# A selective scan layer whose preparation runs in halves of channels and tokens, with loads waited for later and the last sums ahead of the output products

## The reference

```python
x = x + _L2_attn_ref(_layernorm(x), ...)     # _L2_attn_ref adds its input too:
residual = x
xn = layernorm(x) * ln_w + ln_b
x_inner, z = split(xn @ W_in.T)              # 256 channels each
u = silu(causal_conv4(x_inner) + conv_b)     # 4 taps along 64 tokens of a sequence
dt_low, B_ssm, C_ssm = split(u @ W_x.T)      # 64 + 16 + 16
dt = clip(softplus(dt_low @ W_dt.T + b_dt) + 0.001, 0.001, 0.1)
h_t = exp(-dt_t * exp(log_A)) * h_{t-1} + dt_t * u_t * B_t   # 16 states a channel
y = sum_n(h * C) + u * D_param
return (y * silu(z)) @ W_out.T + residual
```

## Time and profile before

| what | us |
|---|---|
| median of three timed runs (3036.95 to 3038.14) | 3037.8 |
| profiled execution, device time | 3035.6 |
| its span | 3033.8 |
| the scan layer in it, from its first instruction to the last write of `x` | 2196.7 to 2490.3 |
| its loop, from the first scan | 2303.3 to about 2475 |

### The profile page before, as it was taken

One profiled execution on the slowest core, in us unless ns is written; L12 is line 12 of the kernel. 1 busy time (PEld: TensorE's weight loads), 2 busy tenths in 40 slices (PEclk: granted clock), 3 DMA queues, 4 the chain that ended last, 5 costly groups with the idle time before them and its releaser, 6 DMA issues. The chain is left out here.

```text
span 3033.8 us, 66495 instructions
## 1 busy us (share of the span) xinstructions
...
## 2 busy tenths in 40 slices
...
DMA packets 73344, 189.00 MB, mean 62 GB/s; under 512 B 12130, under 2 KB 39717, under 8 KB 73008
## 3 DMA queue, kind: packets, MB, share of 16 engines
...
q0 software_dynamic: 1024, 1.85, 0.2%
...
## 5 line engine op out<-in xcount | busy, mean ns | idle before, releaser
L3062 DVE CUSTOM_DVE_ANT_0 L_xattn_junk<-L_xattn_ps_mx,L_xattn_shift 128x512 f32<-128x512 f32 (+1 forms) x1024 | 545.1, 570 | 112.3 <-issue 102.1
L3143 ACT ACTIVATE L_xattn_pT<-L_xattn_ps_st 128x512 f32<-128x512 f32 x768 | 417.0, 594 | 402.4 <-PE L_xattn_ps_st L2901 402.4
L2914 PE MATMUL L_xattn_ps_mx<-L_xattn_kT,L_xattn_qb 32*128 32x512 f32 (+1 forms) x2048 | 480.0, 551 | 0.0
L2901 PE MATMUL L_xattn_ps_st<-L_xattn_qb,L_xattn_kT 32*128 32x256 f32 (+1 forms) x3328 | 454.5, 383 | 0.0
L3108 DVE TENSOR_TENSOR L_xattn_pT<-L_xattn_pT,L_xattn_capT 128x512 f32<-128x512 f32 (+1 forms) x710 | 423.2, 637 | 29.8 <-ACT L_xattn_pT L3143 26.8
L2901 PEld LDWEIGHTS L_xattn_ps_st<-L_xattn_qb,L_xattn_kT 32*128 32x128 f32 (+1 forms) x3328 | 299.3, 180 | 18.5
L2961 PE MATMUL L_xattn_ps_pv<-L_xattn_pT,L_xattn_v 128*17 128x128 f32 x6656 | 263.0, 276 | 0.0
L2961 PEld LDWEIGHTS L_xattn_ps_pv<-L_xattn_pT,L_xattn_v 128*17 128x17 f32 x6656 | 146.1, 96 | 163.3 <-issue 76.1
L2927 PE MATMUL L_xattn_ps_st<-L_xattn_less,L_xattn_ones_b 3*128 3x512 bf16 x768 | 177.8, 385 | 0.9 <-ACT L_xattn_pT L3143 0.7
L2868 POOL TENSOR_TENSOR L_xattn_qb<-ln_sq,L_xattn_four 128x256 f32<-128x256 f32 x32 | 19.6, 615 | 1089.0 <-PE L_xattn_ps_st L2901 1069.3
L2914 PEld LDWEIGHTS L_xattn_ps_mx<-L_xattn_kT,L_xattn_qb 32*128 32x128 f32 x2048 | 151.5, 183 | 23.9 <-DVE L_xattn_tops L3062 14.6
...
## 6 DMA issues: line engine op xcount, KB each, us to landing
...
```

The costliest lines, as they stand in the source:

```text
L2901: last = nc.tensor.matmul(st[0:chunk[j], w % 3, 256 * c2:256 * c2 + 256], kT[n % 3][r:r + 32, P * j:P * j + chunk[j]], qb[n % 3][r:r + 32, ...
L2914: last = nc.tensor.matmul(mx[:, w % 3, to:to + width], qb[n % 3][32 * g:32 * g + 32, 2 * (p % 2):2 * (p % 2) + 2, :].rearrange("p h q -> p ...
L3062: last = nc.vector.tensor_tensor_reduce(out=junk[:, w % 3, to:to + width], in0=mx[:, w % 3, to:to + width], in1=shift[:, k0:k0 + width], s ...
L3143: nc.scalar.activation(pT[b % HELD][:, :, gi, :], st[:, w % 3, :].rearrange("p (c k) -> p c k", c=2), ACT.Exp)\
```

## The change

The wait for the loads moves behind the first norm on ScalarE and DVE (PE's stays). The zero fill covers only the first column of each sequence, and `la` and `na` are made much later. All eight `xi` products come before the eight `z` products; DVE copies the first half of the channels, ScalarE the second. `CONV` cuts the convolution into three parts: the first half of the channels over all columns, the second half over columns 0 to 1023, and over the rest. PE runs 24 transposes whose result nobody reads, then the low-rank and step-size products for the first half of the tokens and for the second. Exp, Ln, the clips and the product with `u` go by halves of the tokens. The first two decays come after the first `xs`. At the end all sums stand ahead of the output products, and the skip and gate go in pieces of 512 columns. Which of the copies of `xbc` SP waits for changes with it; the loop is otherwise the same.

```diff
+        by_time = [(hf, i) for i in range(4) for hf in range(HALF)]
+        CONV = [(0, 0, TOK), (1, 0, TK), (1, TK, TOK)]
...
+            sp.wait_ge(*V.at("xbc3"))
+            sp.wait_ge(*A.at("xbc1"))
...
             pe.wait_ge(loaded, 160)
 
-            order = [(blk, i) for pair in (0, 1) for i in range(4) for blk in (pair, 2 + pair)]
-            for n, (blk, i) in enumerate(order):
+            for n, (hf, i) in enumerate(quads):
                 if n >= 4:
-                    pe.wait_ge(*(V.at(f"xi{(n - 4) // 2}") if blk < 2 else A.at(f"z{(n - 4) // 2}")))
-                nc.tensor.matmul(ps[:, (0 if blk < 2 else 2) + i % 2, :], win[:, P * blk:P * blk + P], hT[:, 512 * i:512 * i + 512],
+                    pe.wait_ge(*V.at(f"xi{n - 4}"))
+                nc.tensor.matmul(ps[:, n % 4, :], win[:, P * hf:P * hf + P], hT[:, 512 * i:512 * i + 512],
                                  start=True, stop=True).then_inc(PE.did(f"in{n}"), 1)
-            pe.wait_ge(*A.at("u1"))
-            for i in range(4):
+            for n, (hf, i) in enumerate(quads):
+                if n >= 4:
+                    pe.wait_ge(*A.at(f"z{n - 4}"))
+                nc.tensor.matmul(ps[:, 4 + n % 4, :], win[:, P * (2 + hf):P * (2 + hf) + P], hT[:, 512 * i:512 * i + 512],
+                                 start=True, stop=True).then_inc(PE.did(f"z{n}"), 1)
+            pe.wait_ge(*A.at("xi7"))
+            for _ in range(24):
+                nc.tensor.transpose(ps[:, 0, 0:P], c.ident[:, :], c.ident[:, :])
+
+            def low_rank(i):
...
-                    pe.wait_ge(*(A if i % 2 else V).at(f"xbc{i - 2}"))
+                    pe.wait_ge(*A.at(f"xbc{i - 2}"))
...
-            pe.wait_ge(*V.at("xbc2"))
...
+            def step_sizes(n):
+                hf, i = by_time[n]
                 if n >= 4:
                     pe.wait_ge(*V.at(f"pre{n - 4}"))
                 nc.tensor.matmul(ps[:, n % 4, :], wdt[:, P * hf:P * hf + P], xbc[0:R, 512 * i:512 * i + 512],
                                  start=True, stop=True).then_inc(PE.did(f"dt{n}"), 1)
+
+            pe.wait_ge(*A.at("u1"))
+            low_rank(0)
+            low_rank(1)
+            for n in range(4):
+                pe.wait_ge(*A.at(f"xbc{n // 2}"))
+                step_sizes(n)
+            pe.wait_ge(*A.at("u2"))
+            low_rank(2)
+            low_rank(3)
+            for n in range(4, 8):
+                pe.wait_ge(*V.at(f"xbc{n // 2}"))
+                step_sizes(n)
...
             total(K - 1, 0)
+            total(K - 1, 1)
             pe.wait_ge(*G.at("gate0_1"))
             pe.wait_ge(*V.at(f"scan{K - 1}_0"))
             out(0)
             out(1)
-            total(K - 1, 1)
-            pe.wait_ge(*V.at("gate1_1"))
+            pe.wait_ge(*V.at("gate1_1_0"))
             out(2)
+            pe.wait_ge(*V.at("gate1_1_1"))
             out(3)
...
         def _(dve):
-            dve.wait_ge(*A.at("la"))
-            nc.vector.tensor_scalar(na[:, :, :], la[:, :, :], -1.0, None, ALU.mult).then_inc(V.did("na"), 1)
-            nc.vector.memset(da[:, :, :, :], 0.0).then_inc(V.did("da_zero"), 1)
             ln_vector(c, dve, V, A, PE, tp, n1)
+            dve.wait_ge(loaded, 160)
             ln_vector(c, dve, V, A, PE, tp, n2)
...
+            nc.vector.memset(da[:, :, :, :].rearrange("p u h (b q) -> p (u h b) q", q=S)[:, :, 0:1], 0.0).then_inc(V.did("da_zero"), 1)
+            for n in range(4):
+                dve.wait_ge(*PE.at(f"in{n}"))
+                nc.vector.tensor_copy(xi[:, 0, 512 * n:512 * n + 512], ps[:, n, :]).then_inc(V.did(f"xi{n}"), 1)
+            dve.wait_ge(*V.at("xi3"))
+            for m, (hf, lo, hi) in enumerate(CONV):
+                if m == 1:
+                    dve.wait_ge(*A.at("xi7"))
+                x3, u3 = seq(xi[:, hf, lo:hi]), seq(cv[:, hf, lo:hi])
+                nc.vector.tensor_scalar(cv[:, hf, lo:hi], xi[:, hf, lo:hi], taps[:, hf, 3:4], cb[:, hf:hf + 1], ALU.mult, ALU.add)\
+                    .then_inc(V.did(f"cv{m}3"), 1)
...
-            for i in (0, 2):
-                dve.wait_ge(*PE.at(f"xbc{i}"))
-                nc.vector.tensor_copy(xbc[:, 512 * i:512 * i + 512], ps[0:R + 2 * N, 4, :]).then_inc(V.did(f"xbc{i}"), 1)
...
+            def biased(n):
+                hf, i = by_time[n]
...
-            dve.wait_ge(*A.at("ln"))
-            nc.vector.tensor_scalar(dt[:, :, :], dt[:, :, :], DT_MIN, DT_MIN, ALU.add, ALU.max).then_inc(V.did("low"), 1)
-            dve.wait_ge(*V.at("low"))
-            nc.vector.tensor_scalar(dt[:, :, :], dt[:, :, :], DT_MAX, None, ALU.min).then_inc(V.did("dt"), 1)
-            dve.wait_ge(*V.at("dt"))
...
+            for n in range(4):
+                biased(n)
+            for i in (2, 3):
+                dve.wait_ge(*PE.at(f"xbc{i}"))
+                nc.vector.tensor_copy(xbc[:, 512 * i:512 * i + 512], ps[0:R + 2 * N, 4 + i % 2, :]).then_inc(V.did(f"xbc{i}"), 1)
+            for n in range(4, 8):
+                biased(n)
+            dve.wait_ge(*A.at("la"))
+            nc.vector.tensor_scalar(na[:, :, :], la[:, :, :], -1.0, None, ALU.mult).then_inc(V.did("na"), 1)
             for th in range(TH):
                 at = slice(TK * th, TK * th + TK)
+                dve.wait_ge(*A.at(f"ln{th}"))
+                nc.vector.tensor_scalar(dt[:, :, at], dt[:, :, at], DT_MIN, DT_MIN, ALU.add, ALU.max).then_inc(V.did(f"low{th}"), 1)
+                dve.wait_ge(*V.at(f"low{th}"))
+                nc.vector.tensor_scalar(dt[:, :, at], dt[:, :, at], DT_MAX, None, ALU.min).then_inc(V.did(f"dt{th}"), 1)
+                dve.wait_ge(*V.at(f"dt{th}"))
                 nc.vector.tensor_tensor(xi[:, :, at], dt[:, :, at], cv[:, :, at], ALU.mult).then_inc(V.did(f"dtu{th}"), 1)
...
-            for hf in range(HALF):
-                skip(1, hf)
-                dve.wait_ge(*V.at(f"skip1_{hf}"))
-                nc.vector.tensor_tensor(half(xi, hf, 1), half(xi, hf, 1), half(zs, hf, 1), ALU.mult).then_inc(V.did(f"gate1_{hf}"), 1)
+            for i in (0, 1):
+                at = slice(TK + 512 * i, TK + 512 * i + 512)
+                for hf in range(HALF):
+                    dve.wait_ge(*PE.at(f"y{K - 1}_{hf}"))
+                    nc.vector.scalar_tensor_tensor(out=xi[:, hf, at], in0=cv[:, hf, at], scalar=dp[:, hf:hf + 1], in1=ps[:, 2 * hf + i, :],
+                                                   op0=ALU.mult, op1=ALU.add).then_inc(V.did(f"skip1_{hf}_{i}"), 1)
+                for hf in range(HALF):
+                    dve.wait_ge(*V.at(f"skip1_{hf}_{i}"))
+                    nc.vector.tensor_tensor(xi[:, hf, at], xi[:, hf, at], zs[:, hf, at], ALU.mult).then_inc(V.did(f"gate1_{hf}_{i}"), 1)
...
+            ln_scalar(c, act, V, A, PE, tp, n1)
             act.wait_ge(loaded, 160)
+            ln_scalar(c, act, V, A, PE, tp, n2)
+            for n in range(4, 8):
+                act.wait_ge(*PE.at(f"in{n}"))
+                nc.scalar.copy(xi[:, 1, 512 * (n - 4):512 * (n - 4) + 512], ps[:, n - 4, :]).then_inc(A.did(f"xi{n}"), 1)
+            for n, (hf, i) in enumerate(quads):
+                act.wait_ge(*PE.at(f"z{n}"))
+                nc.scalar.activation(zs[:, hf, 512 * i:512 * i + 512], ps[:, 4 + n % 4, :], ACT.Silu).then_inc(A.did(f"z{n}"), 1)
+
+            def convolved(m):
+                hf, lo, hi = CONV[m]
+                act.wait_ge(*V.at(f"cv{m}0"))
+                nc.scalar.activation(cv[:, hf, lo:hi], cv[:, hf, lo:hi], ACT.Silu).then_inc(A.did(f"u{m}"), 1)
+
+            def low_rank(i):
+                act.wait_ge(*PE.at(f"xbc{i}"))
+                nc.scalar.copy(xbc[:, 512 * i:512 * i + 512], ps[0:R + 2 * N, 4 + i % 2, :]).then_inc(A.did(f"xbc{i}"), 1)
+
+            convolved(0)
+            convolved(1)
+            low_rank(0)
+            convolved(2)
+            low_rank(1)
             nc.scalar.activation(la[:, :, :], la[:, :, :], ACT.Exp).then_inc(A.did("la"), 1)
-            ln_scalar(c, act, V, A, PE, tp, n1)
-            ln_scalar(c, act, V, A, PE, tp, n2)
-            for n, (hf, i) in enumerate(quads):
-                act.wait_ge(*PE.at(f"in{2 * n + 1}"))
-                nc.scalar.activation(zs[:, hf, 512 * i:512 * i + 512], ps[:, 2 + i % 2, :], ACT.Silu).then_inc(A.did(f"z{n}"), 1)
-            for hf in range(HALF):
-                act.wait_ge(*V.at(f"cv{hf}0"))
-                nc.scalar.activation(cv[:, hf, :], cv[:, hf, :], ACT.Silu).then_inc(A.did(f"u{hf}"), 1)
-            for i in (1, 3):
-                act.wait_ge(*PE.at(f"xbc{i}"))
-                nc.scalar.copy(xbc[:, 512 * i:512 * i + 512], ps[0:R + 2 * N, 5, :]).then_inc(A.did(f"xbc{i}"), 1)
-            act.wait_ge(*V.at("pre7"))
-            nc.scalar.activation(dt[:, :, :], dt[:, :, :], ACT.Exp).then_inc(A.did("e"), 1)
-            act.wait_ge(*A.at("e"))
-            nc.scalar.activation(dt[:, :, :], dt[:, :, :], ACT.Ln, bias=1.0).then_inc(A.did("ln"), 1)
-            act.wait_ge(*PE.at("bt"))
```

(35 more changed lines are left out.)

29 lines of the change are left out of this document (4 added, 25 removed).

## The result

The changed kernel takes 2999.7 us, the median of four executions (2996.7 to 3004.0), against 3038.0 for the kernel before (3037.0 to 3038.7): a ratio of 0.9876, with a 95% interval of 0.9860 to 0.9891. Forecast were 2998.7 and a range of 2996 to 3002.5. The profiled execution took 2998.9, its span is 2996.3. In it the scan layer, from its first instruction to the last write of `x`, takes 254.8 us (2198.5 to 2453.3) instead of 293.6: 38.8 less, where 39.1 were forecast.

What follows compares the result with a forecast made beforehand. Before the loop a chain of waiting engines bounds the time; inside it three engines are full. Savings of 36.2 us before the loop and 2.9 at the tail, 39.1, from 3037.8 gave 2998.7 us, range 2996 to 3002.5.

Steps and rivals of the forecast that it cites:

- The head: Start of the scan layer: without the wait for loads and the full fill, first statistics start 11.4 us earlier.
- The convolution: After the input products: with all `xi` products first, the first half's convolution starts 9.5 us sooner after the products' start.
- Low rank and step sizes: Products after the convolution: low-rank groups and step-size products at 0.86 us each, DVE's last addition ending at 2249.5 us.
- Halves of tokens: Before the loop: Exp and Ln hidden beneath additions; half-column clips 1.25 us each, product with `u` 2.25, ending at 2254.5.
- The tail: End of the layer: last sums before output groups, skip and gate in 512-column pieces, saving 2.9 us.
- the rival on the clock: First low-rank groups at 1.2 GHz, about 2.7 us later, or first four input products, 3.4 later; 17% together.
- The pause behind table loads: ScalarE pauses 1.28 us after every table load, making its Exps and Lns the path: 3.3 us later, 2%.
- The slower case: The loop starts and stays a while at half clock, about 5 us more per state; ten states give 3048.7; 1%.

## Why the prediction was right

- **The head**, 11.4 forecast: 11.36 in the trace, 11.2 by undoing it. The loads were in before the second norm asked.
- **The convolution**, 9.5 forecast: 9.4, by undoing it and in the trace. ScalarE's Silus hid as said.
- **Low rank and step sizes**: the last addition ends 53.4 us into the layer, not 52.8. The first two groups take 3.67 instead of 3.44, but that is hidden: `xbc1` waits for the third Silu and is ready 43.1 us in, where 43.2 was forecast. Step-size products 2 and 3 then end 0.4 late, and the eight products behind them take 7.3 us instead of 7.0. The clips, the product and the decays give 0.3 back, and the second `xs` misses its forecast by 0.3.
- **Halves of tokens**: undoing them costs 11.1 beside the clock, by a path worked out at 10.7. The 11.1 rests on a price of 1.3 for the clock that was measured in other executions.
- **The tail**, 2.9 forecast: 2.9, twice.
- The three large parts and the tail give 11.2 + 9.4 + 11.1 + 2.9 = 34.6 of the 38.8. The other 4.2 were not undone by themselves; the four low-rank groups alone take 7.3 us instead of 10.0. One part of the change works against it: the decays behind `xs0`, whose place I took into the sum (8.8 us between the first two `xs`, 8.73 measured) without asking whether the old place was better, cost 1.6.
- **The step that was mis-sized** is the chance of the rival on the clock. I gave it 17% for two places together; the low-rank groups lost it in three of seven executions, and the input products in one of thirteen (the executions of the changed kernel and its variants). The idling was 1.9 us, not 1.4, since the 24 transposes took 2.78 us and not 3.1. The price was overrated: 1.3 us where the clock was lost for part of the groups, and 2.3 without the transposes, not 2.7. The profile that the forecast is held against happened to be one without the loss: luck.
- The pause behind table loads is not there: 0.01 and 0.02 us pass (2254.36 + 1.28 to 2255.65, 2264.50 + 1.28 to 2265.80).
- The slower case did not come: 0.99 over the loop.
- That the forecast is 1.0 us off the median is in part luck. The profiled execution is 2.4 us above the 2996.5 that I put beside it: 0.3 in the layer and 1.9 in the cross-attention before it, both in its span, 0.5 of which came back behind the layer, and 0.8 outside the span. The median stands 0.7 above that execution, and not 2.2 as it did before, which hides 1.5 of it.
